# Decoder, two layers: the masked attention's first head pair is stacked by TensorE on the chip instead of through HBM

## What is computed

```python
x = _layernorm(x + _L0_attn_ref(x, ...))    # 16 heads, rotary, difference of two softmaxes
x = _layernorm(x + _L0_xattn_ref(x, ctx_768, ...))
x = _layernorm(x + _L0_ffn_ref(x, ...))     # 8 experts, one per token
x = _layernorm(x + _L1_attn_ref(x, ...))    # 16 heads of 8, causal mask
x = _layernorm(x + _L1_xattn_ref(x, ctx_768, ...))   # 16 heads of 64
x = _layernorm(x + _L1_ffn_ref(x, ...))     # 16 experts, top 4
...
score = jnp.einsum('bhsd,bhtd->bhst', q, k)
score = jnp.where(causal[None, None], score, -jnp.inf)
attn = jax.nn.softmax(score / jnp.sqrt(8.0), axis=-1)
y = jnp.einsum('bhst,bhtd->bhsd', attn, v)
```

## Time and profile before

| | |
|---|---|
| median of 3 executions | 503.17 us (502.87 to 504.73) |
| the profiled execution, its time | 505.22 us |
| the profiled execution, its span | 503.5 us |
| mean granted clock of TensorE | 0.96 of full |
| busy: TensorE, VectorE, ScalarE, GpSimd | 461.6, 269.0, 236.9, 124.7 us |
| 199 to 217 us (before D's first score) | TensorE 15.2 us busy of 18.0 |
| 217 to 227.4 us (D's scores before step 0) | TensorE 9.9 us busy of 10.4 |
| 227.4 to 254.2 us (D's steps 0 to 5) | TensorE 26.7 us busy of 26.8 |

### The profile page before, as it was taken

The page is one execution under the profiler, slowest core; times in us unless marked ns, Lnnn a source line. Parts: engine busy times, 40 slices in busy tenths (PEclk is TensorE's granted clock), DMA queues, the critical chain, the costliest instruction groups (busy, mean ns, idle before and its releaser), DMA issues.

```text
span 503.5 us, 10963 instructions
## 1 busy us (share of the span) xinstructions
PE 461.6 (92%) x4113; PEld 331.9 (66%) x4114; DVE 269.0 (53%) x684; ACT 236.9 (47%) x466; POOL 124.7 (25%) x251
## 2 busy tenths in 40 slices
PE   9698999989679999979988899998989999999993
PEld 3164777766445995446757577887967777667773
DVE  4825678734782536756745688875133432233236
ACT  2942677762130522505563578888216234433340
POOL 4202345432200022215662445334010000000001
PEclk9698999999959999989999999999999899999997
DMA  6866555223310000474111000100000011111111
GB/s 171 296 204 134 143 146 157 84 77 126 111 57 0 1 3 1 148 180 130 52 29 44 12 21 11 52 2 1 1 2 22 22 31 42 42 42 34 29 33 42
DMA packets 23308, 34.41 MB, mean 68 GB/s; under 512 B 7600, under 2 KB 16000, under 8 KB 23008
## 3 DMA queue, kind: packets, MB, share of 16 engines
q1 hardware_dynamic: 23264, 33.81, 23.0%
HBM read 28.26 MB, written 5.24 MB: 67 GB/s over the span
## 4 chain that ended last, share of the span: by engine, by line
PE 76%; DVE 8%; DMA 7%; ACT 4%; issue 2%; SPq 1%; POOL 1%; POOLq 0%; DVEq 0%; ACTq 0%
PE ps L1086 11%; PE ps L1069 11%; PE ps L639 4%; PE ps L665 4%; PE ps L628 4%; PE ps L617 3%; PE ps L988 3%; PE ps L1012 3%; PE ps L1057 3%; PE ps L999 3%; PE ps L959 3%; PE ps L973 2%; PE ps L882 2%; PE ps L677 2%; ACT arena L1134 2%; PE ps L916 2%
## 5 line engine op out<-in xcount | busy, mean ns | idle before, releaser
L1422 DVE TENSOR_REDUCE negm<-ps 128x4 f32<-128x512 f32 x96 | 64.0, 688 | 32.6 <-PE ps L628 31.6
L1134 ACT ACTIVATE arena<-ps,w1a 128x512 f32<-128x512 f32 x64 | 43.4, 687 | 60.6 <-PE ps L1069 59.4
L1744 DVE SCALAR_TENSOR_TENSOR racc<-ps,sm,racc 128x128 f32<-128x128 f32 x128 | 35.9, 344 | 64.8 <-PE ps L1086 64.8
L1134 ACT ACTIVATE probs<-ps 128x512 f32<-128x512 f32 (+1 forms) x100 | 56.4, 592 | 28.4 <-PE ps L639 27.2
L1086 PEld LDWEIGHTS ps<-w1a,arena 128*128 128x128 f32 x512 | 61.0, 196 | 7.2 <-issue 6.2
L1086 PE MATMUL ps<-w1a,arena 128*128 128x128 f32 x512 | 61.4, 280 | 0.8 <-DVE racc L1735 0.8
L1069 PE MATMUL ps<-xT,w1a 128*128 128x512 f32 x128 | 57.9, 594 | 1.4 <-ACT xT L1134 1.4
L1134 ACT ACTIVATE arena<-ps 128x512 f32<-128x512 f32 (+4 forms) x71 | 40.3, 591 | 36.7 <-PE ps L882 15.9
L552 POOL TENSOR_SCALAR rstd<-mv 128x4 f32<-128x4 f32 x12 | 2.7, 227 | 180.2 <-DVE mv L1472 180.2
L596 POOL TENSOR_TENSOR probs<-probs,rzE 128x480 f32<-128x480 f32 x32 | 30.9, 986 | 38.3 <-DVE rzE L1681 38.3
L617 PE MATMUL ps<-onesb 128*128 128x512 bf16 x124 | 37.4, 432 | 3.1 <-DVE sm L1601 2.1
(11 more groups left out here) (211 smaller groups left out, 829.1 us busy)
## 6 DMA issues: line engine op xcount, KB each, us to landing
stackA<-arena SPq DMA_DIRECT2D x12, 256.0 KB, 4.1
arena<-stackA SPq DMA_DIRECT2D x24, 96.0 KB
arena<-stackA SPq DMA_DIRECT2D x8, 288.0 KB
w1a<-in_w1a SPq DMA_DIRECT2D x1, 2048.0 KB, 8.7
w2a<-in_w2a SPq DMA_DIRECT2D x1, 2048.0 KB, 7.5
w1a<-in_w1b SPq DMA_DIRECT2D x16, 128.0 KB, 2.1
w1a<-in_w2b SPq DMA_DIRECT2D x16, 128.0 KB, 2.0
stackD<-arena SPq DMA_DIRECT2D x6, 256.0 KB
```

Of the source, the lines that this page charges most:

```text
L1134: return nc.scalar.activation(o, i, f, **kw)
L1422: nc.vector.tensor_reduce(negm[:, slot % 2, 4 * g:4 * g + 4], tiles(bank(BANK_S + g % 2), 4, P), AX.X, ALU.max, negate=True).then_inc(a.ma ...
L1744: last = stt(racc[:, b, :], bank(banks + half)[:, k * P:(k + 1) * P], sm[:, 11, bass.ds(b * E1 + e, 1)], racc[:, b, :], ALU.mult, ALU.add)
```

## The change

1. **First pair's stack (D).** GpSimd makes a table `pickD` of zeros and ones, long before. With it TensorE picks the 72 rows of pair 0's stack out of the parts: 24 bf16 matmuls of 512 columns (3 parts, queries and keys, 4 pieces of 512 columns each), into all eight banks. ScalarE copies the four pieces of the queries, VectorE the four of the keys, to the stack in SBUF. SyncE still writes all parts to HBM, and reads back only pair 1 at once; pairs 2, 3 and 4 are read behind the move of pair 0's maxima.
2. **Order on TensorE (D).** The values' projection and the keys' projection of all 8 pairs now stand behind or between the scores of pair 0. The keys use four banks in place of six; from pair 4 on ScalarE copies both halves. `head_maxima` of pair 0 stands behind the keys of pair 4.
3. **Start of the steps.** In A and in D the scores of heads 0 and 1 now come from `first_head` and `second_heads`. In A `head_maxima` of head 1 moves from step 0 to before it, its copy goes ahead of step 0's exponentials, and 6 fillers stand in place of 8. In D the first two banks of pair 2 (`third_head`) and `head_maxima` of pair 1 are in step 0, behind its first two `scores_t`, and the 8 fillers are gone, as are the 4 behind the banks of pair 0.

The diff, cut to what sets the order and the waits (the renamed semaphores, the counts that follow from them and the move of `maxima` out of `heads` are left out):

```diff
+        def key_bank(n, half):
+            return BANK_T + 2 * (n % 2) + half
+        def keys_copied(n, half):
+            return n + 1 if n < PAIRS // 2 else 2 * n + half + 1 - PAIRS // 2
...
-                sp.wait_ge(fixed, 3 if count == NH else 10)
-                for n in range(AHEAD):
+                sp.wait_ge(fixed, 3 if count == NH else 13)
+                first = (AHEAD if not a.built else 3 if a is A else 2)
+                for n in range(a.built, first):
                     load_stacks(a, n, n, base, count)
                 sp.wait_ge(zeros, 2 if count == NH else 3)
                 for n in range(count):
                     move_maxima(a, n, n % RING)
+                    if n == 0:
+                        for m in range(first, AHEAD):
+                            load_stacks(a, m, m, base, count)
                     m = n + AHEAD
                     if m < count:
...
             for n, (tile, value) in enumerate((
                     (onesb[:], 1.0), (ones_near, ONES_PAIR), (ones_late, ONES_PAIR),
                      (one[:], 1.0), (mhalf[:], -0.5), (vB[:, :, P:P + 1], 1.0), (vs[:], 0.0),
-                    (vs[:, :, :, :, 16:17], 1.0))):
+                    (vs[:, :, :, :, 16:17], 1.0), (pickD[:], 0.0))):
                 nc.gpsimd.memset(tile, value).then_inc(fixed, 1)
                 pool.wait_ge(fixed, n + 1)
...
+                rows = identb[:, first:first + step * HD:step]
+                for p in range(PARTS):
+                    pch(nc.gpsimd.tensor_copy(table[:, 0, p, p * PARTS * HD:(p + 1) * PARTS * HD].rearrange(
+                        "k (d r) -> k d r", r=PARTS), along(rows, PARTS)))
...
+            for c in range(2):
+                pick(pickD[:, c], c, 2).then_inc(fixed, 1)
...
+            def second_heads(a, causal):
+                pe.wait_ge(a.stack[1], loaded(a, 1))
+                for g in range(4):
+                    scores(a, 1, 1, g, causal)
+                    if g == 1 and not a.built:
+                        head_maxima(a, 0, 0)
+                    keep_busy(1 if causal else 2, BANK_O)
+                if not a.built:
+                    third_head(a, causal)
+                    keep_busy(6, BANK_O)
+            def third_head(a, causal):
+                pe.wait_ge(a.stack[2], loaded(a, 2))
+                scores(a, 2, 2, 0, causal)
+                scores(a, 2, 2, 1, causal)
+                head_maxima(a, 1, 1)
+            def first_head(a, causal):
+                pe.wait_ge(a.stack[0], loaded(a, 0))
+                for g in range(4):
+                    scores(a, 0, 0, g, causal)
+                    keep_busy(1 if causal else 2, BANK_O)
...
                         scores_t(a, n, slot, 1)
+                    if n == 0 and a.built:
+                        third_head(a, causal)
                     if not late_head(n + 2, count):
                         scores(a, n + 2, second, 2, causal)
-                    if not late_head(n + 1, count):
+                    if n > 0 and not late_head(n + 1, count):
                         head_maxima(a, n + 1, ahead)
...
-                for h in range(2):
-                    pe.wait_ge(a.stack[h], (a.turns + 1) * 16 * LOADS)
-                    for g in range(4):
-                        scores(a, h, h, g, causal)
-                        keep_busy(1 if causal else 2, BANK_O)
-                        if h == 1 and g == 1:
-                            head_maxima(a, 0, 0)
-                pe.wait_ge(a.stack[2], (a.turns + 1) * 16 * LOADS)
-                scores(a, 2, 2, 0, causal)
-                scores(a, 2, 2, 1, causal)
-                keep_busy(8, BANK_O)
...
-                    i = 2 * n + half
-                    if i >= KEY_BANKS:
-                        pe.wait_ge((e_kc, e_kd)[half], n - KEY_BANKS // 2 + 1)
-                    mm(bank(BANK_M0 + i % KEY_BANKS)[:, 0:480], wkE[:, n, :], ctxT[:, half * 480:(half + 1) * 480],
+                    if n >= 2:
+                        if half == 1 and n - 2 < PAIRS // 2:
+                            pe.wait_ge(e_kd, n - 1)
+                        else:
+                            pe.wait_ge(e_kc, keys_copied(n - 2, half))
+                    mm(bank(key_bank(n, half))[:, 0:480], wkE[:, n, :], ctxT[:, half * 480:(half + 1) * 480],
                        start=True, stop=True).then_inc(e_k, 1)
...
+            first_head(A, False)
+            second_heads(A, False)
             heads(A, NH, pair=False, causal=False)
...
-            for half in range(2):
+            pe.wait_ge(fixed, 11)
+            for p in range(PARTS):
+                for t in range(2):
+                    pe.wait_ge((D.hi, D.mid, D.lo)[p], t + 1)
+                    for i in range(4):
+                        c, half = divmod(i, 2)
+                        last = mm(bank(4 * t + i)[0:ROWS, :], pickD[:, c, t, p, :], part[:, t, p, half * HALF:(half + 1) * HALF],
+                                  start=p == 0, stop=p == PARTS - 1)
+                        if p == PARTS - 1:
+                            last.then_inc(piece, 1)
+            def masked_values(half):
                 for k in range(4):
                     b = 4 * half + k
-                    last = mm(bank(6 + half)[:, k * P:(k + 1) * P], xT[:, b * P:(b + 1) * P], wvD[:], start=True, stop=True)
+                    last = mm(bank(half)[:, k * P:(k + 1) * P], xT[:, b * P:(b + 1) * P], wvD[:], start=True, stop=True)
                 last.then_inc(D.vps, 1)
-            pe.wait_ge(D.full, 2)
-            for n in range(PAIRS):
-                project_keys(n)
-            pe.wait_ge(e_kc, PAIRS)
-            pe.wait_ge(e_kd, PAIRS)
+            pe.wait_ge(piece_sb, D.piece0 + 8)
+            scores(D, 0, 0, 0, True)
+            scores(D, 0, 0, 1, True)
+            project_keys(0)
+            scores(D, 0, 0, 2, True)
+            project_keys(1)
+            scores(D, 0, 0, 3, True)
+            masked_values(0)
+            masked_values(1)
+            project_keys(2)
+            project_keys(3)
+            project_keys(4)
+            pe.wait_ge(D.vall, 1)
+            head_maxima(D, 0, 0)
+            project_keys(5)
+            project_keys(6)
+            project_keys(7)
+            pe.wait_ge(e_kc, keys_copied(PAIRS - 1, 1))
+            pe.wait_ge(e_kd, PAIRS // 2)
             pe.wait_ge(D.vall, 2)
-            pe.wait_ge(D.full, 2)
+            second_heads(D, True)
             heads(D, PAIRS, pair=True, causal=True)
             pe.wait_ge(resb, 2)
...
-                    if not late_head(n + 1, count):
+                    if (n > 0 or a.built) and not late_head(n + 1, count):
                         copy_maxima(n + 1, (slot + 1) % RING)
...
-                copy_maxima(0, 0)
+                if not a.built or a is A:
+                    copy_maxima(0, 0)
+                if not a.built:
+                    copy_maxima(1, 1)
                 for n in range(count + 1):
                     step(n, n % RING)
...
-            for n in range(PAIRS):
-                act.wait_ge(e_k, 2 * n + 1)
-                fn(kE[n][:, 0:4, :], tiles(bank(BANK_M0 + 2 * n % KEY_BANKS), 4, L), ACT.Copy).then_inc(e_kc, 1)
+            for i in range(4):
+                c, half = divmod(i, 2)
+                act.wait_ge(piece, D.piece0 + i + 1)
+                fn(queries_of[0][0:ROWS, c, half * HALF:(half + 1) * HALF], bank(i)[0:ROWS, :], ACT.Copy).then_inc(piece_sb, 1)
+            def copy_keys(n, half):
+                act.wait_ge(e_k, 2 * n + half + 1)
+                fn(kE[n][:, 4 * half:4 * half + 4, :], tiles(bank(key_bank(n, half)), 4, L), ACT.Copy).then_inc(e_kc, 1)
+            for n in range(PAIRS // 2):
+                copy_keys(n, 0)
+            copy_keys(4, 0)
+            copy_keys(4, 1)
+            act.wait_ge(D.mt, 1)
+            fn(mT[:, 0, :], maxima_bank[0:PARTS * 16, :], ACT.Copy).then_inc(D.mc, 1)
+            for n in range(5, PAIRS):
+                copy_keys(n, 0)
+                copy_keys(n, 1)
             heads(D, PAIRS)
...
+                for h in range(1 if a is D else 0, 2):
                     for g in range(4):
-                        maxima(h, h, g)
+                        maxima(a, h, h, g)
...
-            for half in range(2):
+            for i in range(4):
+                c, half = divmod(i, 2)
+                dve.wait_ge(piece, D.piece0 + 4 + i + 1)
+                nc.vector.tensor_copy(keys_of[0][0:ROWS, c, half * HALF:(half + 1) * HALF], bank(4 + i)[0:ROWS, :]
+                                      ).then_inc(piece_sb, 1)
+            def copy_keys(n):
+                dve.wait_ge(e_k, 2 * n + 2)
+                nc.vector.tensor_copy(kE[n][:, 4:8, :], tiles(bank(key_bank(n, 1)), 4, L)).then_inc(e_kd, 1)
+            def copy_values(half):
                 dve.wait_ge(D.vps, half + 1)
-                tt(vall[:, 4 * half:4 * half + 4, 0:P], tiles(bank(6 + half), 4, P), over(bvD[:], 4), ALU.add).then_inc(D.vall, 1)
```

(19 more changed lines are left out.)

56 lines of the change are left out of this document (33 added, 23 removed).

## The result

| | before | changed |
|---|---|---|
| executions measured side by side | 503.95 us (median of 4) | 509.18 us (median of 4, 508.35 to 511.79) |
| ratio | | 1.0115 (1.0065 to 1.0165) |
| the profiled execution, its time | 505.22 us | 511.79 us |
| its span | 503.5 us | 510.1 us |

The changed kernel is slower, by 5.8 us (3.3 to 8.3) according to the ratio; the forecast was +4.5 us, 507.7 us. The interval lies above the 0.5% that the prediction took as distinguishable from no change.

The account below looks back on a forecast made before the run. TensorE was taken to bound D, the masked attention. +3.5 us to step 1, +1.7 for the clock and -0.7 in A, the first attention, gave +4.5 on the 503.17 median: 507.7 us, range 503.8 to 510.4.

Parts of the forecast that it names:

- VectorE's four pieces: Before D's first score: VectorE copies four 72x512 key pieces from PSUM, 0.66 us each, 2.7 us in all.
- standstill ahead of the first score: In D, TensorE stands still between the last picking matmul, 206.7, and the first score, 209.0: 2.3 us.
- (a): Ahead of pair 1's scores in D, TensorE waits for the last keys to be copied: 0.9 us.
- (b): In D's step 0, turning pair 1's maxima waits for its last maximum and GpSimd's split: 1.0 us standstill.
- (c): In D, pair 1's maxima move behind three stack reads on SyncE: nothing, up to 1 us if queued behind their data.
- the other rows up to step 1: In D: scores 6.3 us, `scores_t` 0.9, two turnings of maxima 0.3, fillers 1.7.
- step 1 at full clock: D's step 1 at 235.2 against 231.7 before, +3.5 us, with no fall of the clock counted.
- The keys are moved, not shortened.: In D, key matmuls (13.3 us) and values (1.8 us) now stand behind the first score, at unchanged length.
- The rival by which the chain decides: In D, keys fit in the relay's gaps, so step 1 moves with the first score, -8.0: 494.5 us; chance 0.05.
- The clock, +1.7: Behind D's first score, TensorE's clock falls as before, costing scores and keys 1.7 us; range 0 to 3.4.
- The rival "the clock holds": In D, no clock fall and small waits, 1.2 in place of 1.9 us: 505.3 us; chance 0.19.
- A, -0.7: First attention: moving head 1's maxima earlier and dropping two fillers brings step 1 0.7 us sooner; bounds 0 and -1.3.

Follow-up runs that it names:

- runs 2: Next sublayer's key matmuls and their copies left out of both old and changed kernel; the next sublayer's first scores: 86.52 us old, 80.19 changed, from D's projections' start.
- The run of A alone: Old kernel with only the first attention's (A's) edits: 6 fillers for 8, head 1's maxima turned and moved before step 0; 504.37 us, ratio 1.0016.
- D's part alone: Changed kernel with the start of A, the first attention, put back as before, keeping the masked attention's (D's) edits; 507.78 us, ratio 1.0117.
- the whole, second profile: The changed kernel, unaltered, timed and profiled again beside the old kernel; 507.99 us, ratio 1.0111, the profiled execution 516.38 us.
- both waits filled: Old kernel with 7 more fillers in D's wait for pair 0's stack and 7 in A's wait for head 2's stack; 502.58 us, ratio 0.9963.
- values in the gap: Changed kernel with the values' 16 matmuls moved into TensorE's standstill between the picking matmuls and the first score; 506.34 us, ratio 1.0041.
- changed at its best: Changed kernel with the values' matmuls before the first score, without D's 12 fillers, and 7 fillers in A's wait for head 2's stack; 505.15 us, ratio 1.0004.
- the run with D's wait filled: Old kernel with 7 more fillers in D between the last key matmul and the wait for pair 0's stack; 502.56 us, ratio 0.9972.
- the fillers out: Old kernel with 13 fewer fillers in D and pair 1's maxima turned and moved before step 0; 503.31 us, ratio 0.9997.

## Why the prediction was right, and where it was not

The side, the place and the mechanism were right, and the total was near; two of its terms were wrong, and they worked in opposite directions. That the total came so near is in part luck: without the two terms the prediction's sum is +3.5 us, close to the +3.04 of the profiles, and the 1.0 us that they add stands in for a part of the measured loss that no profile shows.

| step of the prediction | forecast, us | measured in the profile after |
|---|---|---|
| first score, from the projections' start | 13.4 | 13.22 |
| VectorE's four pieces | 2.7 (4 x 0.66) | 2.48 (4 x 0.62) |
| standstill ahead of the first score | 2.3 | 1.93 |
| keys and values | 15.1 | 15.2 (1.66 + 1.66 + 1.84 + 4.92 + 5.10, from start to start, without the wait of 0.66) |
| waits (a), (b), (c) | 0.9, 1.0, 0 | 0.66, 0.42, 0 |
| the other rows up to step 1 | 9.2 | 9.7 |
| step 1 at full clock | 39.6 | 39.16 |
| the clock | +1.7 | 0 |
| A | -0.7 | 0 |

- **Start of pair 0's scores, and what stands behind it.** Right to 0.5 us at step 1 (235.2 - 195.57 = 39.6 against 39.16). It was a count of rows times durations of rows, and held for that reason. The term of 0.216 us for a matmul of 512 columns held: twelve picks in 2.78 us, of which the last takes 0.38 to its end, leave 0.218 for each. The Trainium skill's 131 ns ("TensorE: Matmul & The Clock Gate", back-to-back issue gap) is not seen in this stream either.
- **"The keys are moved, not shortened."** Right, and the point on which all hangs: runs 2 show 13.3 us that cost nothing where they stood, and 8.0 where they stand now. The rival by which the chain decides (494.5) put its threshold at more than 8 of 15.1 us of keys and values in gaps. Of the keys 5.3 us lie in gaps.
- **Waits.** (a) and (b) are where they were put, at 1.08 together against 1.9. (c) is 0 before step 1, as forecast.
- **The clock, +1.7: wrong.** I gave the new kernel the old one's fall because its standstill, 2.3 us, seemed as long as the 2.41 of the earlier trace rows. It was 1.93, behind picks that end at 210.35, and in all three profiles of the changed D the clock stayed at 1.00. The reason itself, that a standstill as long brings the same fall, does not hold either: the changed kernel without keys stood still for 3.07 us and kept 1.00. So the old kernel's fall is gone, which is a gain, and step 1 is later by 3.04 us and not by 5.2. The distance that the prediction named as its test, from the end of the projections to step 1, is 35.6 us counted in its way, against 37.8 forecast and 32.6 before. The rival "the clock holds" had this and the small waits right (1.08 us, it said 1.2) and forecast 505.3, a D of +2.8; it describes the profile better than the forecast does, though the executions' time lies nearer to the forecast.
- **A, -0.7: wrong, at its bound of 0.** The working freed the move of head 1's maxima from its place behind step 0 and took its landing for granted 2.3 us later; in the profile after it took 6.1. The bound of 0 was given for another wait, that step 0's own move ends it, and this is there as well, 0.44 us. The run of A alone has step 1 at 49.61, 0.66 sooner than before, yet no gain in time, 504.37; the first profile of the whole has it at 50.33, as late as before. And where the clock does not fall in A, old and changed order reach step 2 at the same time, 50.31 (D's part alone) and 50.34 (the whole, second profile).
- **The total.** By these profiles the change is +3.04, while the medians of executions say +3.9 to +5.2, and the three ratios 1.0111 to 1.0117 with a lower bound of 1.0065, 3.3 us. The forecast of +4.5 lies in the middle, but the profiles show no road to it. What stays open is 1 to 2 us. It does not lie behind D, where the old kernel, the two profiles of the whole and those of its two parts all have 222.8 to 222.9 us left. But other profiles (both waits filled, values in the gap, changed at its best) have 221.2 there, and lack a fall of the clock that the former have near 400 us. So falls far from the change move a time by 1.6 us, and one kernel's executions may have them more often than another's; that is not shown. Another possible cause, not shown either: the old kernel's fall in D may be missing in part of its unprofiled executions. With the fall away, as in the run with D's wait filled, the old kernel would be at 84.2 and the difference 4.0. It was there in all three profiles that have the old wait unfilled and the keys ahead of it: the old kernel's, that of A's part alone and that with the fillers out. For the kernels of the table the difference of medians follows "next" to within some 2 us, and that is as far as one profiled execution carries here.

## What to carry to other kernels

Read a transfer's cost as its bare part only: this round trip took 11.7 us, and 9.3 of them lay beside work that had to be done anyway; when a change makes a transfer shorter, ask first what that work will lie beside afterwards. On the engine that is the bound, a ledger of distances between two fixed rows settles such a question to 0.2 us where the whole time scatters by some per cent; then a run with the cover taken out of both kernels says who pays for it. Of the two ways to deal with the bare wait, filling it gained 0.9 us of "next" here (1.2 with A's filled too; the ratios, 0.9972 and 0.9963, hardly leave 1), while taking it away with new matmuls on the engine that is the bound, and with the old ones moved out of its cover, lost 3.0.

## What the runs showed of the hardware that was not expected

- **A small move can take far longer to land while large reads run.** The same move of maxima landed 2.3 us behind its issue at a DMA share of 0.11 in the windows, and 6.1 us behind it at 0.78 to 0.82 (5.8 with A's part alone: issued at 43.84, step 1 released at 49.61). It need not: in the second profile of the changed kernel it was issued at 43.70, and step 1 began without a wait at 47.92, so it took 4.2 us at most, at 0.69 to 0.76.
- **Fillers held the clock where a short standstill lost it, and the length of a standstill alone does not tell.** The clock fell behind standstills of 2.41, 2.76 and 2.26 us at the same place of the old order (old kernel, A's part alone, fillers out) and behind one of 1.21 us with the fillers taken out. It did not fall in the three profiles in which seven fillers (1.67 us) stood in that place, nor behind 1.93 us in the changed kernel, nor behind 3.07 us in the changed kernel without keys.
- **The same kernel loses its clock in different places.** The start of D's projections was at 199.06 us in one profile of the changed kernel, at 203.4 in the other, at 194.64 with D's part alone and at 208.17 without keys, while the distances inside D held. A fall near 400 us was there in eight of the thirteen profiles, and its being there or not is worth 1.6 us. Executions of the old kernel in one session lay between 498.93 and 524.35 us.
- **Copies of 72x512 from PSUM, 32-bit to bf16**, took 0.62 us on VectorE and 0.51 on ScalarE, less than the 0.66 of 128x480 and 0.60 of 128x512 in the earlier trace rows.
